# Second attention: the next step's scores ahead of the weighted sum on TensorE

## What is computed

```python
qkv = hidden_states @ qkv_w + qkv_b          # 4 batches x 256 tokens, 32 heads of 16
q = _rope(q, cos, sin); k = _rope(k, cos, sin)
scores = jnp.einsum('bqhd,bkhd->bhqk', q, k) * scale
scores = scores + (1.0 - causal) * MASK_VAL
probs = jax.nn.softmax(scores, axis=-1)
ctx = jnp.einsum('bhqk,bkhd->bqhd', probs, v).reshape(b, s, e)
return ctx @ out_w + out_b
```

## Time and profile before

| | us |
|---|---|
| median of 3 runs | 1855.64 (1850.51 to 1855.73) |
| the profiled execution | 1852.38 |
| its span in the trace | 1850.6 |
| second attention, first scores to last weighted sum | 1534 to 1768 |
| PE busy over the whole span | 1754.1 (95%) |
| DVE, ACT, POOL busy | 1114.3, 1085.9, 913.0 |

### The profile page before, as it was taken

One profiled execution on the slowest core, in us unless ns is written; L12 is line 12 of the kernel. 1 busy time (PEld: TensorE's weight loads), 2 busy tenths in 40 slices (PEclk: granted clock), 3 DMA queues, 4 the chain that ended last, 5 costly groups with the idle time before them and its releaser, 6 DMA issues.

```text
span 1850.6 us, 32124 instructions
## 1 busy us (share of the span) xinstructions
PE 1754.1 (95%) x11088; PEld 1523.0 (82%) x11088; DVE 1114.3 (60%) x3334; ACT 1085.9 (59%) x3075; POOL 913.0 (49%) x1154
## 2 busy tenths in 40 slices
PE   7989999999999999999999999999999788898778
PEld 6789989989998999998999899899877665666556
DVE  6664465465456556556645655654666777777666
ACT  3365566566567565656655665655642536777843
POOL 5455445555445554555544455545522436668710
PEclk9999999999999999999999999999999998999999
DMA  4300011011012002101200200110120310000001
GB/s 149 114 12 7 18 58 35 1 58 52 1 30 69 13 11 65 35 1 46 64 1 19 75 18 7 57 47 1 35 63 17 105 38 1 2 2 24 19 6 46
DMA packets 35424, 65.78 MB, mean 36 GB/s; under 512 B 4032, under 2 KB 4672, under 8 KB 35264
## 3 DMA queue, kind: packets, MB, share of 16 engines
q1 hardware_dynamic: 35264, 63.73, 11.3%
HBM read 61.62 MB, written 2.10 MB: 34 GB/s over the span
## 4 chain that ended last, share of the span: by engine, by line
PE 72%; DVE 9%; ACT 8%; issue 6%; POOL 4%; DMA 0%; POOLq 0%; SPq 0%; DVEq 0%; ACTq 0%
PE bank L362 56%; PE bank L995 6%; PE bank L982 4%; PE bank L997 3%; ACT s L1109 2%; POOL s L1832 2%; DVE h L689 1%; PE bank L1515 1%; ACT s L1601 1%; PE bank L1544 1%; PE bank L1531 1%; DVE work L1214 1%; POOL rstd L327 1%; ACT pt L1594 1%; POOL W L271 1%
## 5 line engine op out<-in xcount | busy, mean ns | idle before, releaser
L362 PE MATMUL bank<-W,oT 128*128 128x512 f32 x1632 | 431.4, 400 | 1.0 <-DVE oT L1784 1.0
L1320 POOL TENSOR_TENSOR qk<-work,qk 128x512 fp32r<-128x512 f32 (+1 forms) x160 | 193.3, 1208 | 429.2 <-ACT qk L1100 429.2
L362 PEld LDWEIGHTS bank<-W,oT 128*128 128x128 f32 x1632 | 289.3, 189 | 49.2 <-issue 1.3
L1116 ACT COPY pt<-bank 128x384 f32<-128x384 f32 x256 | 122.0, 477 | 322.8 <-PE bank L982 322.1
L1312 POOL TENSOR_TENSOR work<-work,table 128x512 f32<-128x512 f32 (+1 forms) x160 | 191.3, 1196 | 135.4 <-ACT work L1095 135.4
L1109 ACT ACTIVATE s<-s,neg_max 128x128 f32<-128x128 f32 (+1 forms) x512 | 227.6, 446 | 49.9 <-DVE neg_max L1228 48.8
L362 PE MATMUL bank<-W,xnA 128*128 128x320 f32 (+1 forms) x1056 | 186.5, 333 | 3.4 <-DVE xnA L347 2.8
L362 PEld LDWEIGHTS bank<-W,xnA 128*128 128x128 f32 x1056 | 166.6, 188 | 16.9 <-DVE xnA L347 4.0
L1205 DVE TENSOR_TENSOR work<-bank,table 128x512 f32<-128x512 f32 (+1 forms) x160 | 102.0, 637 | 130.0 <-ACT work L1095 129.8
L362 PE MATMUL bank<-qk 128*128 128x256 f32 (+1 forms) x768 | 166.0, 351 | 0.9 <-POOL qk L1320 0.9
L362 PE MATMUL bank<-xnB,W 128*128 128x256 f32 (+1 forms) x1080 | 163.3, 301 | 3.5 <-DVE xnB L347 3.5
(11 more groups left out here) (105 smaller groups left out, 3503.4 us busy)
## 6 DMA issues: line engine op xcount, KB each, us to landing
raw<-in_weights SPq DMA_DIRECT2D x215, 256.0 KB, 2.7
x<-in_x SPq DMA_DIRECT2D x8, 256.0 KB, 4.8
out<-x SPq DMA_DIRECT2D x8, 256.0 KB, 2.0
row<-in_bias_rows SPq DMA_DIRECT2D x5, 256.0 KB, 2.9
table<-in_constants SPq DMA_DIRECT2D x4, 240.0 KB, 3.0
b_qk<-in_bias_rows SPq DMA_DIRECT2D x1, 512.0 KB, 4.9
b_val<-in_bias_rows SPq DMA_DIRECT2D x1, 256.0 KB, 2.9
table<-in_constants SPq DMA_DIRECT2D x1, 66.0 KB, 2.4
```

What stands on the lines that cost most here:

```text
L362: last = nc.tensor.matmul(out_ap, lhs(i), rhs(j), start=start and k == 0, stop=stop and k == 2)
L1116: nc.scalar.copy(pt0[:, k, :], bank[PT][:, 0:3 * P]).then_inc(a_pt, 1)
L1320: nc.gpsimd.tensor_tensor(lo, work[:, 2 + s, st.columns(what)], hi.bitcast(F32), ALU.subtract).then_inc(a_rope_lo, 1)
```

## The change

In `b_tensor_step` the call that issues the next step's scores stands ahead of the call that issues the weighted sum of the step in front, where it stood behind it. Nothing else differs: the same instructions, the same waits on each, and the other engines' programs are the same row for row.

```diff
                     b_tensor_project(pe, b, i)
                 else:
                     b_tensor_out(pe, b, i, bank[FILL])
+            if n + 1 < QUADS:
+                b_tensor_scores(pe, n + 1)
             if n >= 1:
                 weigh(n - 1)
-            if n + 1 < QUADS:
-                b_tensor_scores(pe, n + 1)
             if n < QUADS:
                 turn(n, 0)
                 turn(n, 1)
```

## The result

The changed kernel takes 1861.75 us (median of 6 runs, 1860.49 to 1864.59), the kernel before 1854.03 on the same chip (6 runs, 1850.51 to 1858.15). The ratio is 1.0047, 95% interval 1.0030 to 1.0064: 8.7 us slower, between 5.6 and 11.9. The profiled execution took 1860.52, its span is 1858.7, against 1852.38 and 1850.6.

A forecast was written before the change was run, and what follows sets the result against it. PE is 95% busy overall, but here a chain of waits through DVE, ACT and PE was taken as the bound. Terms 1.62 + 0.53 + 0.87 + 1.74 + 0.87 + 0.80 = 6.4 us on 1855.64 gave 1862.0, range 1855 to 1868.

The forecast's parts named there:

- The carrier: Even steps behind a fill: the later weighted sum delays ACT's oT, DVE's low part, minima and exponentials by 0.87 us.
- The rival of the DVE chain alone: Delay passes only where the chain already lies on DVE, steps 4, 14, 22, 30: 3.4 us, 1859.0; chance 0.19.
- that of filled waits: Scores fill waits in steps 26, 28 and 6, gaining 3.3 us, slack swallows the rest: 1852.3; chance 0.08.
- that of no effect: Nothing moves, since PE's transposes don't: 1855.6; chance 0.05.
- s = 2 and step 12: Steps 2, 10, 18 and 12: late reciprocal delays POOL and PE's head 3; 0.54 us each, 0.53 in step 12.
- Step 4: Step 5 has no fill and PE waits for ACT's queries, with no slack between: 0.87 us lost.
- Steps 14 and 22: DVE's add and moments follow oT; minima, exponentials, queries and PE's next pair hang on them: 0.87 us each.
- s = 0: Steps 8, 16, 24: PE's key and query transposes wait for oT's low part; 0.31 us twice, 0.25 in step 24.
- Step 30: Later oT delays DVE's minima of step 31 and the end of the attention: 0.80 us.
- step 20: POOL splits weight chunks, then normalises all four heads without a wait, so late exponentials cost 0.
- Batch 3 without fill: Steps 25 to 28: queries or POOL still hold PE, so scores first gain 0.
- the clock falls in step 15 and around step 23: Rival: the delay goes through and PE's clock also falls there, 9.2 us in all, 1864.8; chance 0.13.

The follow-up runs named there:

- early minima: Changed kernel, with DVE taking the next step's minima of heads 0 and 1 ahead of the low part of oT in even steps: 1853.01 us, ratio 0.9987.
- the filled kernel before: Kernel before, plus six matmuls nobody reads ahead of the pair in steps 5, 6 and 25 to 28: 1854.16 us, ratio 1.0005.
- the dummy work: Changed kernel, plus six matmuls nobody reads ahead of the pair in steps 5, 6 and 25 to 28: 1858.22 us, ratio 1.0024.

## Why the prediction was right, and where it was off

*The carrier.* Right: the weighted sum of even steps, ACT's oT, DVE's low part, the minima (in s = 0 PE's transposes instead). Three experiments agree: even steps alone cost all, odd steps nothing, and early minima take the loss away. The rival of the DVE chain alone (3.4 us) falls by the terms behind steps 2, 8, 10, 12, 16 and 18, that of filled waits and that of no effect by the ratio.

*s = 2 and step 12, 0.54 predicted, 0.41 measured.* The steps of the sum held, the sizes shrank: DVE's L1692 took 0.70 instead of 0.76, so the exponentials came 0.83 later and not 0.87; the reciprocal had 0.16 to spare (0.83 - 0.67) rather than 0.13; and head 3 started 0.30 ahead of the fill instead of 0.33.

*Step 4, 0.87.* The step itself gave 0.64, for the 0.16 of the shorter gap behind the queries; another 0.36 came up at step 6, where I had said 0 since DVE came to oT late. With even steps alone the two are 0.80 and 0. So the term is right together and its place is not; what the swap of step 5 does to step 6 was not followed up. The pair of step 6 ran at full clock in the changed kernel and at 1.2 GHz in the first profile of before, but that is not it: in the second profile of before it ran at full clock too, and the pairs 5 to 7 kept their distance within 0.1.

*Steps 14 and 22, 0.87 each, measured 0.70 and 0.67.* The chain moved by 0.87, as predicted (1643.12 - 1639.77 - 2.48), and PE waited 2.38 us for the queries instead of 1.94. I had overlooked that the scores, now first, start 0.16 sooner behind the queries than the weighted sum did.

*s = 0, 0.31, measured 0.42.* DVE's low part of step 16 started where I put it: 1659.27 - 3.18 = 1656.09. PE's L1486 then started 0.15 behind its end (1659.27 + 0.42 = 1659.69 to 1659.84), where I had taken 0.06 from POOL's case, and the fill behind it moved by the same 0.42 (1662.30 - 1658.70 - 3.18).

*Step 30, 0.80, and step 20, 0.* Right within 0.1 in the changed kernel. *Odd steps, 0:* nothing lost, but for the 0.16 gained behind the queries.

*Batch 3 without fill, 0.* This is the step that failed: 2.7 us in all three executions. I had looked for a loss of clock in steps 15 and 23, where the wait grew. In step 15 the pair behind the wait of 2.38 us ran at full clock (0.94 for the scores). In step 23 it did run at 1.2 GHz (1.65 and 1.51), which cost only 0.40, since part of the scores there had run so before as well (1.25 instead of 0.94). And the clock was low in step 26, from the weighted sum on, and in step 27 (1.67 instead of 0.94 for the scores, 1.48 and 1.51 instead of 0.86 for the weighted sum):

```profile
1649.76 0.94 PE L1515 MATMUL bank<-kT,qz 32*128 32x128 f32 x16 [2.38 <-ACT qz L1584]
...
1710.20 1.65 PE L1515 MATMUL bank<-kT,qz 32*128 32x128 f32 x16 [2.37 <-ACT qz L1584]
1711.77 1.51 PE L1531 MATMUL bank<-pt,vz 128*32 128x256 f32 x16
...
1733.22 0.94 PE L1515 MATMUL bank<-kT,qz 32*128 32x128 f32 x16 [2.23 <-DVE b_neg_max L1743]
1734.09 1.48 PE L1531 MATMUL bank<-pt,vz 128*32 128x256 f32 x16
...
1741.95 1.67 PE L1515 MATMUL bank<-kT,qz 32*128 32x128 f32 x16 [2.74 <-ACT qz L1584]
1743.55 1.51 PE L1531 MATMUL bank<-pt,vz 128*32 128x256 f32 x16
```

The predicted rival (9.2 us, "the clock falls in step 15 and around step 23") was thus near the 8.7 us of the ratio, but mostly by another place. Its own falls come and go: step 15 ran at full clock in both profiles of the changed kernel and at the lower one with even steps alone (1.57) and in the filled kernel before (1.58); step 23 at the lower one in the first profile of the changed kernel and not in the second. So the longer wait in step 15 does not bring the fall by itself, and the old wait does not keep it away. That the 2.7 us of batch 3 are the clock's agrees with the dummy work, behind which these steps ran at full clock and the 2.7 us were gone. That the swap alone brings the fall is not shown: the old order has it too in some executions (2.17 us in one), and a reason why it should come with the swap every time is still open. The Trainium skill ("TensorE: Matmul & The Clock Gate", section "What's actually happening") lets the clock depend on how busy PE has been; the trace of the changed kernel with dummy work agrees between 1720 and 1780 (0.94 instead of 0.82).

*The time.* 1862.0 by the sum against 1861.75 is closer than the reasoning deserves, and partly luck: two errors cancelled. The base was taken 1.6 too high (1855.64; 1854.03 in the runs beside the changed kernel), and the loss 6.4 where 7.7 by the medians, 8.7 by the ratio was measured: some 5.9 of the mechanism, and most of the rest, by the traces, of the clock in batch 3. The signs predicted for the profile came out but one: the shift over the attention was 9.1 and not 6 to 7.

## What to carry to other kernels

When two blocks on a full engine change places, that engine's own schedule says nothing; ask for each block who waits for its end, and follow that engine's queue until something with slack swallows the delay. Put work that nobody waits for soon (here the moments) into an engine's wait and not between a late input and the instruction that others need: that was worth 3.5 us, 0.9 to 6.3, and no order of the pair alone gained anything. And where the matmul engine has gaps, keep a part of the loss apart for the clock, and look at several executions before giving it to the change.

## What the runs showed that I had not expected

- PE took up work 0.15 us after the end of DVE's L1784, and 0.06 after POOL's L1832. Behind ACT's queries it took 0.20 for the block with five waits, 0.14 with the late one last, 0.04 for the block with two.
- The clock makes single executions of the same order differ: from pair 25 to pair 29 by up to 1.3 us in four traces whose kernels don't differ there (before twice, and the swaps in s = 6 and in s = 0 alone), and by 2.17 where only the order of waits does; between the pairs 23 and 24 the shift changes by -0.84 to 0.40, with the swap and without. A term of 0.4 us can be read in a trace, step by step, and not in a total.
- Gaps of 2.2 to 3.1 us were followed by matmuls at full clock in steps 15, 25 and 26 and at 1.2 GHz in steps 23 and 27 of one and the same execution.
- DVE's L1692, which reads two tiles of SBUF, took 0.68 us in step 12 of one execution of the changed kernel and 1.40 in another; POOL's pair beside it took 2.11 and 1.61. Such an exchange moved the next queries by 0.7 us.
